# A two-layer AdaLN transformer block: the order of projections, head duos and row stores in layer 0's local maxima

## What is computed

```
qkv = x @ w_qkv.T                       # q, k, v: 16 heads of 16
kc, vc = chunk n-1 and chunk n of k, v  # chunks of 64
scores = einsum('bhnid,bhnjd->bhnij', qc, kc) / sqrt(16)
scores = where(band and key >= 0, scores, min)   # band: i <= j <= i + 64
out = einsum('bhnij,bhnjd->bhnid', softmax(scores), vc)
```

## Time and profile before

| what | us |
|---|---|
| median of 3 runs | 639.07 (637.02 to 639.45) |
| the profiled execution | 639.43 |
| its span | 637.6 |
| TensorE busy | 593.0 (93%) |
| share of TensorE in the chain that ended last | 70% |
| VectorE busy | 367.7 (58%) |
| ScalarE busy | 291.0 (46%) |
| GpSimd busy | 117.7 (18%) |
| DMA, mean over the span | 70 GB/s |

### The profile page before, as it was taken

The page is one execution under the profiler, slowest core; times in us unless marked ns, Lnnn a source line. Parts: engine busy times, 40 slices in busy tenths (PEclk is TensorE's granted clock), DMA queues, the critical chain, the costliest instruction groups (busy, mean ns, idle before and its releaser), DMA issues.

```text
span 637.6 us, 10169 instructions
## 1 busy us (share of the span) xinstructions
PE 593.0 (93%) x3762; PEld 452.6 (71%) x3762; DVE 367.7 (58%) x693; ACT 291.0 (46%) x450; POOL 117.7 (18%) x90
## 2 busy tenths in 40 slices
PE   4888999998999999999999798889999999999995
PEld 4656545587888888888888565544447788888885
DVE  6357765856344445444557789894376533344556
ACT  3656675554323333333432464338763643333331
POOL 4500022122122211222230000003101231122220
PEclk9998999999999999999999899999999999999999
DMA  8463566000010111111100015312210000111101
GB/s 320 126 224 113 168 225 203 1 2 26 26 49 26 49 49 49 49 49 49 49 25 2 1 52 155 123 38 85 84 38 2 25 26 26 49 49 49 49 1 66
DMA packets 22193, 44.63 MB, mean 70 GB/s; under 512 B 3632, under 2 KB 7632, under 8 KB 22160
## 3 DMA queue, kind: packets, MB, share of 16 engines
q1 hardware_dynamic: 21840, 44.05, 21.7%
q10 hardware_dynamic: 320, 0.13, 0.1%
HBM read 33.16 MB, written 11.01 MB: 69 GB/s over the span
## 4 chain that ended last, share of the span: by engine, by line
PE 70%; DVE 20%; ACT 5%; issue 2%; DMA 2%; POOL 1%; ACTq 0%; SPq 0%; DVEq 0%
PE PS L559 33%; PE PS L1005 15%; DVE nmx L1617 6%; PE PS L888 4%; PE PS L857 2%; PE PS L721 2%; PE PS L836 2%; PE PS L841 2%; DVE stats L1500 1%; PE PS L725 1%; DVE x L1684 1%; PE PS L903 1%; DMA qk_slot<-rows_scr 1%; DVE xn L1829 1%; PE PS L638 1%
## 5 line engine op out<-in xcount | busy, mean ns | idle before, releaser
L1330 ACT ACTIVATE qk_hi<-xn 128x512 fp32r<-128x512 f32 x82 | 51.7, 631 | 166.6 <-DVE xn L1829 137.0
L559 PE MATMUL PS<-h_hi,wqkv_hi 128*128 128x512 f32 x304 | 103.7, 398 | 3.6 <-DVE h_lo L1534 2.0
L559 PE MATMUL PS<-h_hi,wqkv_lo 128*128 128x512 f32 x272 | 92.9, 397 | 1.8 <-DVE xn L1739 1.8
L1826 DVE TENSOR_TENSOR prs<-prs,PS 128x512 f32<-128x512 f32 x60 | 41.2, 687 | 84.8 <-PE PS L559 84.8
L525 POOL TENSOR_TENSOR wqkv_hi<-fw_raw,wqkv_hi 128x768 fp32r<-128x768 f32 x18 | 33.1, 1838 | 250.5 <-ACT wqkv_hi L1306 250.5
L1833 DVE TENSOR_TENSOR qk_lo<-xn,qk_hi 128x512 fp32r<-128x512 f32 x70 | 48.4, 692 | 50.3 <-ACT qk_hi L1330 50.3
L1326 ACT ACTIVATE prs<-PS 128x512 f32<-128x512 f32 x82 | 48.7, 594 | 49.6 <-PE PS L559 49.6
L559 PEld LDWEIGHTS PS<-h_hi,wqkv_hi 128*128 128x128 f32 x304 | 57.5, 189 | 16.3 <-DVE h_lo L1534 2.8
L559 PE MATMUL PS<-h_lo,wqkv_hi 128*128 128x512 f32 x160 | 63.5, 397 | 0.0
L559 PEld LDWEIGHTS PS<-h_hi,wqkv_lo 128*128 128x128 f32 x272 | 51.5, 189 | 13.4 <-DVE xn L1739 2.7
L1005 PE MATMUL PS<-wqkv_hi,qk_hi 128*128 128x256 f32 x280 | 52.1, 285 | 0.9 <-POOL qk_lo L531 0.7
(11 more groups left out here) (266 smaller groups left out, 1149.5 us busy)
## 6 DMA issues: line engine op xcount, KB each, us to landing
fw_raw<-in_ffn SPq DMA_DIRECT2D x41, 384.0 KB, 3.1
qk_slot<-rows_scr SPq DMA_DIRECT2D x32, 200.0 KB
rows_scr<-qk_hi SPq DMA_DIRECT2D x16, 256.0 KB
qk_slot<-q_scr SPq DMA_DIRECT2D x32, 100.0 KB
rows_scr<-qk_lo SPq DMA_DIRECT2D x8, 256.0 KB
wmod<-in_wmod SPq DMA_DIRECT2D x1, 1536.0 KB, 12.8
x<-in_x SPq DMA_DIRECT2D x2, 512.0 KB, 4.3
wmod<-in_wmod SPq DMA_DIRECT2D x1, 1024.0 KB, 9.2
```

What stands on the lines that cost most here:

```text
L559: ins = nc.tensor.matmul(dst, left(a, c), right(b, c), start=n == 0, stop=n == total - 1)
L1330: nc.scalar.activation(hidR[b][0], hid[b], ACT.Copy).then_inc(f["hi"], 1)
L1826: tt(hid[buf] if half is None else gu[buf], gact[buf], PS[:, 5, :], ALU.mult).then_inc(f["gu"], 1)
```

## The change

TensorE's, ScalarE's and VectorE's orders in the local maxima are written out anew; loops over heads become straight code. TensorE now does duo j and beside it one other piece of work: projections 2, 0, 3, 1 (`PROJECTED0`) behind duos 0 to 3, gate steps behind duos 4 to 7, the V products behind duos 8 and 9, shifts and the second gate's steps one by one behind duos 9 to 13. ScalarE masks a duo behind each eviction to `q0F`, and takes batch 1's high rows by four separate calls of `q0_high` (m = 2, 3, 0, 1), each as soon as batch 0's masks (keys) or scores (queries) no longer need the old rows and these have been written out. VectorE makes the low parts behind duos 7, 8, 9 and 10, and `max_low(0, 0)` comes behind duo 11 (it came behind duo 9). `ORDER0[1]` is changed to (2, 3, 0, 1), and so is the order of batch 1's stores.

```diff
@@ -273,7 +273,8 @@
                 "early_hid", "early_lo")})
 
 
-        ORDER0 = ((0, 1, 2, 3), (0, 2, 1, 3))
+        ORDER0 = ((0, 1, 2, 3), (2, 3, 0, 1))
+        PROJECTED0 = (2, 0, 3, 1, 4, 5)
 
         LOOPS = [(TILES[l] - TAIL[l]) // 2 for l in range(2)]
         SPANS = [[(2, LOOPS[0])], [(2, SHT[1] // 2), (SHT[1] // 2, LOOPS[1])]]
@@ -575,14 +576,15 @@
                 ins = shifts(0, j, 7)
             ins.then_inc(mod_ps, 1)
 
-            def shifts_rest0():
-
-                pe.wait_ge(loaded["wmod0b"], 16)
-                pe.wait_ge(v_taken, 2)
-                pe.wait_ge(q0F_ready, 4)
-                for j in range(4, 8):
-                    ins = shifts(0, j, SHIFT_BANK)
-                ins.then_inc(mod_ps, 1)
+            def shifts_rest0(j):
+
+                if j == 4:
+                    pe.wait_ge(loaded["wmod0b"], 16)
+                    pe.wait_ge(v_taken, 2)
+                    pe.wait_ge(q0F_ready, 4)
+                ins = shifts(0, j, SHIFT_BANK)
+                if j == 7:
+                    ins.then_inc(mod_ps, 1)
 
             def shifts1(js):
 
@@ -645,16 +647,17 @@
             BANK0 = ((0, 1, 2, 3, 4, 5), (5, 6, 7, 5, 6, 7))
 
             def project0(b, m):
-                if m == 0:
+                i = PROJECTED0.index(m) if b else m
+                if i == 0:
                     pe.wait_ge(hl_ready, 2 * b + 2)
                     pe.wait_ge(wqkv_ready, 1)
-                if b and m == 0:
+                if b and i == 0:
                     pe.wait_ge(v_taken, 2)
-                if b and m == 4:
+                if b and i == 4:
                     pe.wait_ge(gate_taken, 1)
-                if b and m >= 3:
-                    pe.wait_ge(q0F_ready, m - 2)
-                bank = BANK0[b][m]
+                if b and i >= 3:
+                    pe.wait_ge(q0F_ready, i - 2)
+                bank = BANK0[b][i]
                 if m < 4:
                     product(PS[:, bank, :], lambda a, c: wqkv[a][:, c, m * P:(m + 1) * P],
                             lambda a, c: hR[a][:, c, b, :], KC).then_inc(proj, 1)
@@ -760,28 +763,35 @@
                 nc.tensor.transpose(PS[0:H * NT, MAX_BANK[l], 0:P], nmx[:, b * H * NT:(b + 1) * H * NT], ident[:, :])\
                     .then_inc(a["mt"], 1)
 
-            GATE_HEADS = ((5, 7, 9, 11), (5, 8, 11, 14))
-
-            def local_maxima(beside):
+            def scores_pair0(b, j):
+                scores(0, BQ * b + j // 2, 2 * (j % 2) + 1, b)
+
+            def local_maxima():
 
                 pe.wait_ge(consts, CONSTS)
                 pe.wait_ge(qlo, 4)
-                for b in range(B):
-
-                    if b:
-                        shifts_rest0()
-                    pe.wait_ge(qhi, (4, 6)[b])
-                    for s in range(SLOTS):
-                        scores(0, BQ * b, s, b)
-                        for work in beside[b][s]:
-                            work()
-                    if b:
+                pe.wait_ge(qhi, 4)
+                for j in range(H // 2):
+                    scores_pair0(0, j)
+                    if j < 4:
+                        project0(1, PROJECTED0[j])
+                    else:
+                        gate0_step(0, j - 4)
+                pe.wait_ge(qhi, 4 + 3)
+                for j in range(H // 2):
+                    if j == 4:
+                        pe.wait_ge(qhi, 4 * B)
+                    scores_pair0(1, j)
+                    if j == 0:
                         max_rows(0, 0)
-                        pe.wait_ge(qhi, 4 * B)
-                    for i in range(SLOTS, H):
-                        scores(0, BQ * b + i // SLOTS, i % SLOTS, b)
-                        if i in GATE_HEADS[b]:
-                            gate0_step(b, GATE_HEADS[b].index(i))
+                        project0(1, 4)
+                    elif j == 1:
+                        shifts_rest0(4)
+                        project0(1, 5)
+                    else:
+                        gate0_step(1, j - 2) if j < 6 else None
+                    if 2 <= j < 5:
+                        shifts_rest0(j + 3)
                 filler(4, 6)
                 pe.wait_ge(at[0]["mxd"], 2 * PAIRS - 1)
                 keys_major(0, 0)
@@ -936,13 +946,9 @@
                 norm_transposes(2 * l + 1, (0,))
                 values(l, QUADS - 1, range(NT))
 
-            def next0(*ms):
-
-                return [lambda m=m: project0(1, m) for m in ms]
-
             for m in range(6):
                 project0(0, m)
-            local_maxima(([next0(m) for m in range(4)], [next0(4), [], next0(5), []]))
+            local_maxima()
             values_pass(0)
 
             def out_projection(l):
@@ -1176,18 +1182,11 @@
                 nc.scalar.activation(qm[s][:, :], rows[:, bass.ds(first + head // 2, 1), :].rearrange("p m t -> p (m t)").bitcast(F32),
                                      ACT.Copy, scale=headmask[:, bass.ds(4 * head + s, 1)]).then_inc(a["qm"], 1)
 
-            def mask_first(l, b):
-                act.wait_ge(qhi, (4, 6)[b])
-                act.wait_ge(loaded["headmask"], 16)
-                for s in range(SLOTS):
-                    mask_q(l, b, BQ * b, s)
-
-            def mask_rest(l, b):
-                if l == 0:
-                    act.wait_ge(qhi, 4 * (b + 1))
-                with act.Fori(BQ * b + 1, BQ * (b + 1)) as g:
-                    for s in range(SLOTS):
-                        mask_q(l, b, g, s)
+            def mask_pair0(b, j):
+
+                act.wait_ge(qhi, (3, 5)[b] + j // 4)
+                for h in range(2):
+                    mask_q(0, b, BQ * b + j // 2, 2 * (j % 2) + h)
 
             def exp_table():
                 nc.scalar.activation(table_in[:, :], ct[:, 0, 0, 0:1], ACT.Exp)
@@ -1210,29 +1209,40 @@
             for m in range(4):
                 act.wait_ge(proj, m + 1)
                 nc.scalar.activation(qkR[0][:, m, :], PS[:, m, :], ACT.Copy, scale=SCALE if m < 2 else 1.0).then_inc(qhi, 1)
-            mask_first(0, 0)
+            act.wait_ge(loaded["headmask"], 16)
+            mask_pair0(0, 0)
+            mask_pair0(0, 1)
             take_v(0)
 
-            for m in range(4):
-                act.wait_ge(proj, 6 + m + 1)
-                nc.scalar.activation(q0F[:, m, :], PS[:, (5, 6, 7, 5)[m], :], ACT.Copy, scale=SCALE if m < 2 else 1.0)\
+            def q0_high(m):
+
+                if m < 2:
+                    act.wait_ge(at[0]["s"], H // 2 * (m + 1))
+                else:
+                    act.wait_ge(at[0]["qm"], H // 2 * (m - 1))
+                act.wait_ge(scr0_written[m], 16 * 3)
+                act.wait_ge(q0F_ready, PROJECTED0.index(m) + 1)
+                nc.scalar.activation(qkR[0][:, m, :], q0F[:, m, :], ACT.Copy).then_inc(qhi, 1)
+
+            for i, m in enumerate(PROJECTED0[:4]):
+                act.wait_ge(proj, 6 + i + 1)
+                nc.scalar.activation(q0F[:, m, :], PS[:, (5, 6, 7, 5)[i], :], ACT.Copy, scale=SCALE if m < 2 else 1.0)\
                     .then_inc(q0F_ready, 1)
-            mask_rest(0, 0)
+                mask_pair0(0, 2 + i)
+            mask_pair0(0, 6)
+            q0_high(2)
+            mask_pair0(0, 7)
+            q0_high(3)
+            q0_high(0)
             take_gate(0, 0)
-            act.wait_ge(at[0]["s"], H)
-
-            def q0_high(ms):
-                for m in ms:
-                    act.wait_ge(scr0_written[m], 16 * 3)
-                    act.wait_ge(q0F_ready, m + 1)
-                    nc.scalar.activation(qkR[0][:, m, :], q0F[:, m, :], ACT.Copy).then_inc(qhi, 1)
-
-            q0_high(ORDER0[1][:2])
-            mask_first(0, 1)
-            q0_high(ORDER0[1][2:])
+            mask_pair0(1, 0)
+            mask_pair0(1, 1)
+            q0_high(1)
+            mask_pair0(1, 2)
+            max_high(0, 0)
             take_v(1)
-            max_high(0, 0)
-            mask_rest(0, 1)
+            for j in range(3, H // 2):
+                mask_pair0(1, j)
             exp_table()
             take_gate(0, 1)
 
@@ -1647,27 +1657,26 @@
                     dve.wait_ge(a["oz"], c + 1)
                 nc.vector.tensor_copy(oT[c // OC][0][:, c % OC, :], oN).then_inc(a["oh"], 1)
 
-            def maxima_first(l, b):
-                for s in range(SLOTS):
-                    maxima(l, BQ * b, s)
-
-            def maxima_rest(l, b):
-                with dve.Fori(BQ * b + 1, BQ * (b + 1)) as g:
-                    for s in range(SLOTS):
-                        maxima(l, g, s)
-
             for m in range(4):
                 dve.wait_ge(qhi, m + 1)
                 stt(qkR[1][:, m, :], PS[:, m, :], SCALE if m < 2 else 1.0, qkR[0][:, m, :].bitcast(F32),
                     ALU.mult, ALU.subtract).then_inc(qlo, 1)
-            maxima_first(0, 0)
-            maxima_rest(0, 0)
-            for i, m in enumerate(ORDER0[1]):
-                maxima(0, BQ, i)
-                dve.wait_ge(qhi, 4 + i + 1)
+            def maxima_pair0(b, j):
```

(16 more changed lines are left out.)

## The result

| | before | after |
|---|---|---|
| median, us | 638.05 (635.98 to 639.45, 4 runs) | 645.01 (643.73 to 646.56, 4 runs) |
| profiled execution, us | 639.43 | 644.38 |
| its span, us | 637.6 | 642.5 |
| TensorE's mean granted clock | 0.99 | 0.981 |

The ratio is 1.0113, with a 95% interval of 1.0072 to 1.0153. The forecast was no change, the range ended at 642.4.

The account below looks back on a forecast made before the run. Layer 0's maxima were taken as bound by the rigid 22.5 us from `max_low` to the fifth row pair; -0.65 us from reordering and 1.2 for a clock fall gave +0.55, so 639.6 us median, range 635.0 to 642.4.

Parts of the forecast that it names:

- fall of the clock behind it: TensorE after its idle stretch before duo 8: a clock fall costing 1.2 us, with bounds 0 and 1.7.
- ninth score product (fifth pair): First score product needing the fifth row load (heads 8 and 9), forecast to land at 86.6 us.
- the second fall: TensorE's clock falling again around the score products: work done at 86.2 us, before the fifth pair lands at 86.6.
- the cover: Slack before the fifth pair of rows lands that hides a second clock fall: 0.4 us.
- the prediction's signs of being wrong: `q0_high` not waiting for its rows, or the fifth pair landing under 21 or over 24 us after `max_low`.
- +0.3 us for more instructions to fetch: Unrolled loops of masks and maxima: put at 0, with +0.3 us as the slower end.
- The queue's model: SyncE's DMA queue: the piece from `max_low`'s end to the fifth pair's landing stays rigid at 22.5 us.
- The landing of batch 0's rows: Last store of m = 3 lands at 48.2 us, so ScalarE waits and TensorE idles 3.5 us before duo 8.
- The give-back: Up to `max_low`: 5 us won by duos go to the landing wait and `max_low`'s later place.
- B: TensorE's order decides: first row pairs land early enough, keys start 5.3 us earlier, end near 634; chance 0.15.
- C: Batch 0's rows land before ScalarE asks for them: all shifts by -3.1 us, median 636.0; chance 0.17.
- D: Slower by TensorE's clock alone, falling three times: +3.15 us, 642.3 to 642.6; chance 0.11.

Follow-up runs that it names:

- e1: The changed kernel with 22 filler matmuls instead of 4 ahead of the first score product; 639.81 us, 1.0036 of the kernel before.
- e7: The changed kernel with 16 dense filler matmuls added behind the second score product, inside the slow stretch; 642.44 us, 1.0061 of the kernel before.
- e3: The kernel before with `max_low(0, 0)` behind duo 11 instead of duo 9, VectorE's loop written out; 648.63 us, 1.0166 of the kernel before.
- e9: e3 with 22 fillers instead of 4 in its wait for the first rows; 643.71 us, 1.0119 of the kernel before.
- e8: e4 with 22 fillers instead of 4 in the wait for the first rows; 636.34 us, 0.9971 of the kernel before.
- e6: e5 with the first eight heads' row loads issued before the stores of batch 1's third and fourth row groups; 636.03 us, 0.9975 of the kernel before.
- e5: e4 with `max_low(0, 0)` behind duo 8 instead of duo 11; 629.57 us, 0.9869 of the kernel before.
- e2: The changed kernel with `max_low(0, 0)` behind duo 8 instead of duo 11; 634.01 us, 0.9930 of the kernel before.
- e4: The changed kernel with batch 1's rows in order 2, 0, 3, 1 and duos 8 and 9 masked before m = 3; 638.10 us, 1.0010 of the kernel before.
- e10: The changed kernel with 12 fillers instead of 4 ahead of the first score product; 643.11 us, 1.0083 of the kernel before.

## Why the prediction was wrong

Step by step, measured times less the 1.26 us:

| step | forecast | measured |
|---|---|---|
| the rows of m = 3 are out, `q0_high` goes on | 48.2 | 48.1 |
| idle before duo 8 | 3.5 us | 3.2 us |
| fall of the clock behind it | 1.2 us of 1.7 | 1.7 us of clock lost from 50 to 58 |
| `max_low` ends | 64.15 | 63.7 |
| first score product | 75.6 | 75.4 |
| wait before it | 3 to 4 us | 3.99 us |
| ninth score product (fifth pair) | 86.6 | 89.8 |

**The step that failed** is the price of the second fall: "A fall costs what the old one did: (1 - 0.72) x 6 = 1.7 us", and with it "So a second fall is covered; the cover is 0.4 us." I took one fall's length for the length of every fall. The old one was followed by projections, dense products of 128 rows, and lasted 3.4 us. The second is followed by the values pass, and there it lasted 17 us: (0.27 + 0.50 + 0.50 + 0.50 + 0.36) x 4 = 8.5 us of clock time. From the first to the ninth score product the forecast had 8.9 us of work, 10.6 with the fall; measured were 14.4. By the piece of 22 us behind `max_low` the fifth pair would have let the ninth start near 87; TensorE got there at 91.01, 4 us later, and lost another 0.9 us until the clock came back at 92.9. e1 returned 5.2 us by filling the wait, e7 2.6 us by ending the slow stretch; e3 and e9 show the same in the kernel before, at 3 to 5 us.

A row of the kernel before could have warned. The prediction says that no row before 76 us shows TensorE after 3 us of pure idleness, but it stood idle for the first 8.53 us, and then its 512-column products start 0.43 us apart until 20.8 and 0.23 apart afterwards. Sixteen 2-column products take 3.54 us at 8.53 against 1.84 at 52.09, so that is some 12 us at half speed, short waits included. The column of the granted clock says 1.00 there, so it takes the durations to see it:

```profile
19.50 0.63 PE L559 MATMUL PS<-h_lo,wqkv_hi 128*128 128x512 f32 x1
19.93 0.63 PE L559 MATMUL PS<-h_hi,wqkv_lo 128*128 128x512 f32 x1
...
21.84 0.40 PE L559 MATMUL PS<-h_hi,wqkv_lo 128*128 128x512 f32 x1
22.07 0.40 PE L559 MATMUL PS<-h_hi,wqkv_hi 128*128 128x512 f32 x1
```

Neither of the prediction's signs of being wrong came (`q0_high` waited, and where the fifth pair's landing shows and the DMAs' order is the same, it came 21.6 to 21.9 us behind `max_low`); the term that failed had no sign of its own. The +0.3 us for more instructions to fetch in its bounds has no row behind it, and no run separates it.

*What held.* The queue's model: from the end of `max_low` to the fifth pair's products 22.5 us before, and where TensorE waited for that pair 21.6 (e1, e9) and 21.9 (e8). It held as long as the order of the DMAs did; in e6, with another order, it was 26.5 (52.12 to 78.59). The landing of batch 0's rows, read from the two loads queued behind the last store. The give-back: duos won in batch 0, lost to the wait and to the place of `max_low`.

*The rivals.* B and C did not occur. D had the right engine and the right sign, at chance 0.11, but as three falls of 1.7 us, with the last behind the fifth pair. The rule of the Trainium skill that activity releases the throttle ("TensorE: Matmul & The Clock Gate", section "What's actually happening") agrees with both falls; for the release the trace shows a stretch where TensorE is busy and the clock stays down: 12 of 12 us busy at a clock of 0.50 from 78 to 90. I weighed the rule for whether the clock would fall, and not for how long it would stay. The Trainium skill's 2.0 us beside rival C ("DMA: Bandwidth & Descriptors", section "Anatomy of one DMA — SWDGE (gpsimd) path") is stated there for DMAs that GpSimd issues, and these are SyncE's; C itself goes by the 1.8 us of the earlier trace rows.

*Share of the parts.* The change's order of duos is a gain: with `max_low` behind duo 11 in both, the old order takes 648.63 (e3) and the new one 645.01. With `max_low` early and no mask behind the wait (e5) it is 8.9 us faster than the kernel before; how much of that an early `max_low` would give in the old order, no run shows. Two details turned it: `max_low` two duos later (e2 wins 11.0 us by putting it behind duo 8), and `q0_high(3)` ahead of batch 1's first masks (e4 wins 6.9).

## What to carry to other kernels

Price a stall of TensorE by what comes behind it as well as by its own length: here a 4 us wait ahead of thin products (50 rows or 17 columns) left them at half clock for 14 to 17 us, and fillers in that wait were worth more than they cost. When a stage is sped up, look for the small result that starts the next stage's transfers and move it forward first; an engine that arrives early and must wait can lose more than it won. And in a DMA queue in program order, don't put a wait where a useful transfer could fill it.

## What the runs showed of the hardware

The granted clock stayed at 0.50 for 14 to 17 us in the changed kernel, e3, e4 and e10 while the profile shows TensorE busy from the first score product on, and it came back while 16 dense 512-column matmuls ran (e7). The length differs with the same work, too: behind the wait before duo 8 the clock was low for 3.4 us in the changed kernel and for 6.8 in e2. Idle stretches of about 2 us had either outcome, and one of 1.65 us was followed by a fall (e8). All five waits of 3.2 to 3.9 us before duo 8 (the changed kernel, e1, e2, e7, e10) and all of 3.45 us and more in the values pass were followed by one. A fall may be missed in the mean over the span: 0.990 against 0.981 stand for some 13 and some 24 us at half clock.
